# Sums of down weights made in the last phase, and another order of the closing products

## The reference, cut to what matters

```python
x = x + 0.5 * ffn(layernorm(x))          # x: 4 tiles of 512 tokens, D = 512
x = x + scan_block(layernorm(x))         # matmul, gated scan, layernorm
x = x + 0.5 * ffn(layernorm(x))

def ffn(x):                              # DIM_HIDDEN = 2048, the same weights both times
    gate, up = x @ w_gate.T, x @ w_up.T
    return (silu(gate) * up) @ w_down.T
```

## Time and profile before

| what | value |
|---|---|
| runs | 1024.21, 1025.92, 1026.52 us (median 1025.92) |
| profiled execution | 1023.93 us, span 1022.2 us |
| busy in the span | PE 1010.2, DVE 720.5, ACT 426.6, POOL 193.1 us |
| phases 0, 1, 2, 3 end at about | 260, 521, 783, 1019 us |
| granted clock | 1.000 |

### The profile page before, as it was taken

The page is one execution under the profiler, slowest core; times in us unless marked ns, Lnnn a source line. Parts: engine busy times, 40 slices in busy tenths (PEclk is TensorE's granted clock), DMA queues, the critical chain, the costliest instruction groups (busy, mean ns, idle before and its releaser), DMA issues.

```text
span 1022.2 us, 13275 instructions
## 1 busy us (share of the span) xinstructions
PE 1010.2 (99%) x4796; PEld 849.0 (83%) x4796; DVE 720.5 (70%) x1063; ACT 426.6 (42%) x681; POOL 193.1 (19%) x219
## 2 busy tenths in 40 slices
PE   8999999999999999999999999999999999999998
PEld 7778888877888888888888888888888888888998
DVE  7856685689888787866977887786586444454753
ACT  6645555547333632313824344232273332333530
POOL 4443365306300200210412020003040000000000
PEclk9999999999999999999999999999999999999999
DMA  6589998888666644646756764554577645554255
GB/s 206 205 320 348 358 343 299 311 273 258 231 234 231 221 145 165 208 150 226 250 181 221 234 223 161 180 168 145 182 267 242 216 166 200 209 178 165 94 182 179
DMA packets 73617, 224.21 MB, mean 219 GB/s; under 512 B 6481, under 2 KB 24913, under 8 KB 65873
## 3 DMA queue, kind: packets, MB, share of 16 engines
q1 hardware_dynamic: 72976, 222.33, 63.1%
q10 hardware_dynamic: 576, 1.05, 0.3%
HBM read 168.82 MB, written 54.53 MB: 219 GB/s over the span
## 4 chain that ended last, share of the span: by engine, by line
PE 92%; DVE 3%; DMA 2%; issue 1%; ACT 1%; SPq 1%; POOL 0%; DVEq 0%; ACTq 0%
PE ps_a L1779 8%; PE ps_a L1780 8%; PE ps_a L1781 8%; PE ps_b L1779 7%; PE ps_b L1780 7%; PE ps_b L1781 7%; PE ps_d L1779 7%; PE ps_d L1781 7%; PE ps_d L1780 7%; PE ps_c L1781 6%; PE ps_c L1780 6%; PE ps_c L1779 6%; PE aux L1779 3%; PE aux L1780 3%; PE aux L1781 3%; DMA t_kept<-zx 1%
## 5 line engine op out<-in xcount | busy, mean ns | idle before, releaser
L1203 DVE TENSOR_TENSOR tmp<-tmp,ps_c 128x512 f32<-128x512 f32 x59 | 40.4, 685 | 120.5 <-PE ps_c L1781 120.5
L1779 PE MATMUL ps_a<-xt,gu 128*128 128x512 f32 x304 | 118.4, 390 | 0.6 <-ACT tmp L707 0.6
L1780 PE MATMUL ps_a<-xt,gu 128*128 128x512 f32 x304 | 118.3, 389 | 0.0
L1781 PE MATMUL ps_a<-xt,gu 128*128 128x512 f32 x304 | 118.3, 389 | 0.0
L1779 PE MATMUL ps_b<-xt,gu 128*128 128x512 f32 x286 | 111.5, 390 | 1.3 <-ACT tmp L680 1.3
L1780 PE MATMUL ps_b<-xt,gu 128*128 128x512 f32 x286 | 111.3, 389 | 0.0
L1781 PE MATMUL ps_b<-xt,gu 128*128 128x512 f32 x286 | 111.3, 389 | 0.0
L1779 PE MATMUL ps_d<-dn,hid 128*128 128x512 f32 (+1 forms) x256 | 92.9, 363 | 0.5 <-DVE hid L1248 0.5
L1781 PE MATMUL ps_d<-dn,hid 128*128 128x512 f32 (+1 forms) x256 | 92.8, 363 | 0.0
L1780 PE MATMUL ps_d<-dn,hid 128*128 128x512 f32 (+1 forms) x256 | 92.8, 362 | 0.0
L1781 PE MATMUL ps_c<-xt,gu 128*128 128x512 f32 x236 | 91.8, 389 | 0.0
(11 more groups left out here) (272 smaller groups left out, 2321.2 us busy)
## 6 DMA issues: line engine op xcount, KB each, us to landing
dn<-dn_kept SPq DMA_DIRECT2D x92, 512.0 KB, 3.9
gu<-gu_kept SPq DMA_DIRECT2D x46, 1024.0 KB, 5.1
gu<-gu_kept SPq DMA_DIRECT2D x46, 768.0 KB, 5.1
gu_kept<-gu SPq DMA_DIRECT2D x14, 1024.0 KB, 5.7
gu_kept<-gu SPq DMA_DIRECT2D x14, 768.0 KB, 4.2
dn_kept<-dn SPq DMA_DIRECT2D x16, 512.0 KB, 5.2
t_kept<-zx SPq DMA_DIRECT2D x16, 512.0 KB, 5.8
dn<-t_kept SPq DMA_DIRECT2D x16, 512.0 KB, 3.6
```

The lines of the kernel that those rows point to most:

```text
L1203: dve.tensor_tensor(dst, u3s(si), p5_bank(si)[:, :], ALU.add).then_inc(c22_done, 1)
L1779: pe.matmul(dst, a_hi, b_hi, start=start, stop=False, skip_group_check=chained)
L1780: pe.matmul(dst, a_hi, b_lo, start=False, stop=False, skip_group_check=chained)
L1781: return pe.matmul(dst, a_lo, b_hi, start=False, stop=stop, skip_group_check=chained)
```

## The change

Four things change.

1. The T sums leave phase 0. They are made beside sets 2 to 9 of the last phase (one pair per set) from rows that are loaded again (`load_t_raw`, 512 KB a pair) into free rows of `zx`. POOL's, ACT's, DVE's and SP's parts all move; the store `keep_t` stands between `fetch_dn` and `fetch_b`. There is one buffer for raw rows and one for sums, so pair j waits for pair j-1.
2. `s_of` no longer makes s2; s4 is made in two steps from s3. DVE still has four instructions per pair. s2 is made by POOL, for two pairs at once, in four instructions of 128x1024 (`s2_of`), into `tmp`. `tmp` is in use until the last set's `gated12`, so `s2_of(0)` waits for that.
3. The batches stand in the order of `ENDING`: Q5 quarters 0 and 1, Q6 quarters 0 to 3, Q5 quarters 2 and 3, then Q7, Q3, Q4. The splits follow this order.
4. `d1_hi` no longer waits for the T sums in phase 0, and `load_dn_raw` no longer waits for them; the output stores of tiles 2 and 3 change places.

```diff
+    ENDING = ([(Q5, 0), (Q5, 1)] + [(Q6, i) for i in range(4)] + [(Q5, 2), (Q5, 3)]
+              + [(w, i) for w in (Q7, Q3, Q4) for i in range(4)])
...
+            def load_t_raw(j):
+                if j == 0:
+                    sp.wait_ge(d_done, SEG)
+                wait(sp, t_sums, 4 * j)
+                sp.dma_start(zx_rows[:, 0:2, :], w_ffn_in[2 * j:2 * j + 2, :, 2 * W:2 * W + D].rearrange(
+                    "h p n -> p h n")).then_inc(t_raw_arrived, 16)
...
+                    if p == LAST and 2 <= si < 1 + PAIRS:
+                        load_t_raw(si - 1)
                     if g + 2 < SETS * PH:
                         fetch_a(g + 2)
...
+                    if p == LAST and 2 <= si < 2 + PAIRS:
+                        keep_t(si - 2)
                     if g + 2 < SETS * PH:
                         fetch_b(g + 2)
...
             def d1_hi(p, m):
                 wait(act, d_done, 32 * p + 16 + m - 4 + 1 if m >= 4 else 32 * p)
-                if m < 2 and p == 0:
-                    act.wait_ge(t_lo, PAIRS)
-                if 2 <= m < 4 and p == 0:
-                    act.wait_ge(t_stored, 32 * PAIRS)
+                if m < 4 and p == 0:
+                    act.wait_ge(plain_done, 8)
...
                 act.wait_ge(s_step, 4 * (2 * i + 1) + (2 if w == Q5 else 4))
+                if w == Q6:
+                    act.wait_ge(s2_step, i + 1)
                 act.copy(xt[:, stage_op(n), 0, :, :], stage_rows(w, i)).then_inc(stage_hi, 1)
...
                     copy_u3(g)
+                    if p == LAST and si < 2 + PAIRS:
+                        t_hi_of(si - 2)
...
+            def s2_of(i):
+
+                pool.wait_ge(s_step, 4 * (2 * i + 2))
+                if i == 0:
+                    pool.wait_ge(hid1_done, 16 * PH)
+                    pool.wait_ge(hid21_done, 8 * PH)
+                pool.tensor_tensor(s2_rows(i), hid1[:, 4 * i + 1:4 * i + 4:2, :], first_rows(i, 0), ALU.subtract
+                                   ).then_inc(s2_step, 1)
...
+            for j in range(PAIRS):
+                t_sums_of(j)
+            for i in range(4):
+                s2_of(i)
...
-                dve.tensor_tensor(s2, tile1_odd, s3, ALU.subtract).then_inc(s_step, 1)
+                dve.tensor_tensor(s4, s4, s3, ALU.add).then_inc(s_step, 1)
                 dve.wait_ge(s_step, 4 * q + 3)
-                dve.tensor_tensor(s4, first_row(q, 1), s2, ALU.subtract).then_inc(s_step, 1)
+                dve.tensor_tensor(s4, s4, tile1_odd, ALU.subtract).then_inc(s_step, 1)
...
                 before_c12(p, si)
+                if p == LAST and si < 2 + PAIRS:
+                    t_lo_of(si - 2)
...
-                    pe.wait_ge(block_added, {Q6: 2, Q3: 6, Q7: 8, Q4: 12}[w])
+                    pe.wait_ge(block_added, {Q6: 2, Q3: 8, Q7: 6, Q4: 10}[w])
```

More of the change, by code:

```diff
@@ L255, in by_half, with s2_rows, t_raw @@
             return row.rearrange("p (a n) -> p a n", a=2)
-        def t_raw(j):
-            r = 4 * (j % 2)
-            return zx_rows[:, r:r + 2, :].rearrange("p r (a n) -> p (r a) n", a=2)
+        def s2_rows(i):
+            return tmp[:, 2 * i:2 * i + 2, :]
+        def t_raw():
+            return zx_rows[:, 4:6, :].rearrange("p r (a n) -> p (r a) n", a=2)
         def t_part(part):
@@ L498, in fetch_dn @@
                 else:
[L499 to L501 removed]
+                    w, i = ENDING[n - SEG - PAIRS]
+                    if n < SEG + PAIRS + 4:
+                        sp.wait_ge(t_stored, 32 * (2 * i + 2))
                     if w == Q3:
@@ L617, in _ @@
                     if si == 1:
+                        if p == LAST:
+                            load_t_raw(0)
                         for fetch in (fetch_a, fetch_b):
@@ L798, in t_hi_of @@
                 act.wait_ge(t_sums, 4 * j + 4)
-                if j == 0:
-                    act.wait_ge(plain_done, 8)
                 wait(act, t_stored, 32 * j)
-                act.copy(t_part(0), t_raw(j)).then_inc(t_hi, 1)
+                act.copy(t_part(0), t_raw()).then_inc(t_hi, 1)
             def zw_hi_of(j):
@@ L1006, in _ @@
                         dn_hi_of(si)
-                        if si % 2 == 0:
-                            t_hi_of(si // 2 - 1)
-                        if si == 15:
-                            t_hi_of(7)
                         if 5 <= si < 9:
@@ L1079, in t_sums_of @@
             def t_sums_of(j):
-                even, odd = dn_raw[:, 0, :], dn_raw[:, 1, :]
+                even, odd = zx_rows[:, 0, :], zx_rows[:, 1, :]
                 b11, b12, b21, b22 = even[:, 0:HALF], even[:, HALF:D], odd[:, 0:HALF], odd[:, HALF:D]
-                t = t_raw(j)
-                pool.wait_ge(dn_raw_arrived[0], 16 * (j + 1))
-                pool.wait_ge(dn_raw_arrived[1], 16 * (j + 1))
-                wait(pool, t_lo, j - 1)
+                t = t_raw()
+                pool.wait_ge(t_raw_arrived, 16 * (j + 1))
+                wait(pool, t_lo, j)
                 pool.tensor_tensor(t[:, 0, :], b12, b11, ALU.subtract).then_inc(t_sums, 1)
@@ L1156, in _ @@
                 sums(k)
-                if k % 2 == 0 and k <= SETS:
-                    t_sums_of(k // 2 - 1)
                 if k == 11:
@@ L1333, in add_product @@
             def add_product(w):
-                banks, tile, half, added = {Q5: (z_ps, 3, 1, 0), Q6: (x_ps, 2, 1, 0), Q3: (z_ps, 2, 1, 8),
-                                            Q7: (x_ps, 3, 1, 6), Q4: (x_ps, 3, 0, 0)}[w]
-                add_block(banks, 0, tile, half, bank_done, w + 1, added)
-                add_block(banks, 1, tile, half, batch_done, 4 * w + 4, added)
+                banks, tile, half, added = {Q5: (z_ps, 3, 1, 0), Q6: (x_ps, 2, 1, 0), Q3: (z_ps, 2, 1, 6),
+                                            Q7: (x_ps, 3, 1, 8), Q4: (x_ps, 3, 0, 0)}[w]
+                add_block(banks, 0, tile, half, bank_done, ENDED.index(w) + 1, added)
+                add_block(banks, 1, tile, half, batch_done, ENDING.index((w, 3)) + 1, added)
             def zw_lo_of(j):
@@ L1948, in first_block, with batch @@
                 last.then_inc(first_done, 1)
-            def batch(w, i):
-                m = 4 * w + i
+            def batch(m):
+                w, i = ENDING[m]
                 n = SEG + PAIRS + m
@@ L2139, in _ @@
                 first_block(PAIRS - 1, odd)
-            for w in (Q5, Q6, Q3, Q7, Q4):
-                for i in range(4):
-                    batch(w, i)
+            for m in range(len(ENDING)):
+                batch(m)
 def kernel(**inputs):
```

32 lines of the change are left out of this document (13 added, 19 removed).

## The result

| | before | after |
| --- | --- | --- |
| median of 20 runs each, us | 1023.80 (1022.34 to 1026.52) | 1026.01 (1025.37 to 1026.88) |
| the profiled execution's own time, us | 1023.93 | 1025.42 |
| its span, us | 1022.2 | 1023.6 |
| mean granted clock | 1.000 | 0.997 |
| PE, DVE, ACT, POOL busy, us | 1010.2, 720.5, 426.6, 193.1 | 1009.7, 726.9, 426.2, 201.1 |

The changed kernel takes 1.0021 of the time of the one before (95% interval 1.0015 to 1.0028), so it is 2.2 us slower. The forecast was 1029.5 us: 3.6 (0.35%) above the median of three runs that it started from, 5.7 above the kernel before as 20 runs have it. The direction was right, the size was not.

What follows compares the result with a forecast made beforehand. PE, busy 1010.2 of 1022.2 us, was taken as the bound. Terms -4.95 - 1.1 + 0 + 8.3 + 1.5 = +3.75 us gave 1029.5 us against the median 1025.92; range 1021.0 to 1033.0.

Steps and rivals of the forecast that it cites:

- Third set of phase 0: PE's wait there for ACT, itself held by the store of the pair before, goes: gain 1.5 us.
- last `lo0`: End of phase 0's sets: PE's 0.5 us wait, behind `t_lo` on DVE and `d1_hi` on ACT, goes: gain 0.75 us.
- `d1_lo`: End of phase 0: PE's two waits for its late fifth and sixth parts, 2.2 us, go: gain 2.7 us.
- Phase 0 together: Sum of the three gains in phase 0 from moving the T sums out: -4.95 us.
- Q7 and Q4: Last phase: they share banks and PE idles for the add; with Q3 between them, -1.1 us.
- Sets of the last phase: T sums beside these eight sets fall where DVE and ACT wait for PE: cost 0, bound 10 us.
- the store rival: Last phase: `t_hi_of(j)` waits for the store of j-1, 2 us in each of three sets: 1035.5 us; chance 0.1.
- The gap: Before the third batch, behind the last phase's sets: POOL's s2 instructions hold DVE in turns, PE waits: +8.3 us.
- rivals without the shutting-out: DVE and POOL don't block each other at 1024 elements, or POOL shares; split on time: 1021.1 us, faster; chance 0.12.
- with DVE first: DVE goes first at each hand-over to POOL; adds end +6.2 us, with the clock +7.7: 1027.5 us; chance 0.08.
- The clock: Behind the gap before the third batch PE returns at half clock: +1.5 us, bounds 0 and 1.7.
- The rival in which the clock stays up: DVE and POOL take turns as forecast, but PE's clock does not fall: sum +2.25, 1028.2 us; chance 0.2.

Runs made afterwards that it cites:

- s2 in pieces: Changed kernel with POOL's s2 in 16 instructions of 128x256 in place of four of 128x1024, at the same place: 1022.56 us, 0.9981 of the kernel before.
- the order by product: Changed kernel with each product's four batches in a row (Q5, Q6, Q3, Q7, Q4), so the third batch needs no s2: 1026.08 us, 1.0019 of the kernel before.

## Why the prediction was right or wrong

- **Third set of phase 0, 1.5; last `lo0`, 0.75; `d1_lo`, 2.7.** Each was right: from start to start the three places lost 1.5, 0.7 and 2.7 before, and nothing after. Nothing became late in their stead.
- **Phase 0 together, -4.95.** It was -6.2 by the books and -6.5 with the traces side by side. That is 1.3 to 1.6 too small, and the first failed step: "Behind the start, the waits that the change touches are few." I left out the wait of 0.57 us at 43 us (0.8 with the slow start behind it), because ACT's L707 has no T work near it; POOL's order had to be followed back 20 us to see it. The runs show that it is POOL's eight instructions in a row: with four of them left out it goes, with their order changed it stays. Gaps of 0.1 us in the second half of phase 0, 0.4 together, went too.
- **Q7 and Q4, -1.1.** Right: 1.1 in the trace; 0.9 to 1.3 for the order alone.
- **Sets of the last phase, 0.** Right, and the store rival is refuted: the store of `t_kept` lands in 6.2 us at most, ACT waited for it once, for 0.3 us. (The median of 4.5 us in the earlier trace rows was misread: that answer has the loads from `t_kept` among the stores. The 16 stores of before alone have a median of 5.8, those of after 4.8.)
- **The gap, +8.3.** Right in mechanism, with 7.8 lost. Of its marks one was badly put: POOL's L1110 reads 2.8 to 3.3 us and not 2.4, since its own wait for the turn is in it. 2.4 us a turn were 2.2, since only 0.54 and not 0.60 of a 256-element instruction holds DVE. Three turns of 0.2 make the difference of 0.5. The rivals without the shutting-out (L1333 would be 0.7) and with DVE first (6.2) are refuted.
- **The clock, +1.5.** Right in kind, but 1.8 in the trace is above the bound of 1.7, and 2.7 in another profile far above it: PE does not always come back as it came from the start. The rival in which the clock stays up is refuted by 0.50 in the row above.
- **The sum, +3.75.** By the books it should have been +2.3: 1.3 too little gained in phase 0, 0.5 too much in the gap, 0.3 too little for the clock.
- **From the sum to the time.** The second failed step: "That execution lies 2.0 below the median of the runs shown, so against the median 1025.92 I say 1029.5 us". The median of three runs was 2.1 above that of twenty (1023.80), while the profiled execution (1023.93) was at it. With its own base the sum gives 1027.7, and the right sum 1026.2. Why the three runs lay so high isn't shown, as their clocks aren't on record; in 69 later executions of this kernel the mean granted clock was 0.998 in five, the two slowest (1026.32 and 1026.24 us) among them.

The direction came out right, but not quite for the reason given. I had the gap alone, 8.3 us, outweigh a gain of 6.05. The gap was 7.8 and the gain 7.3 by the books (7.6 side by side), which is nearly even; it is the slow clock behind the gap that made the kernel slower, and with PE kept at work through the gap the difference to the kernel before was gone (0.9996, 0.9987 to 1.0005). So the clock's term decided the sign; in my sum the gap did so by itself. The number itself can't tell the forecast from its rivals: with the right base the rival whose clock stays up would stand at 1026.2, next to the 1026.01 measured, and only the rows refute it.

## What to carry to other kernels

When work is moved to an idle POOL, price it by what DVE does beside it: here each DVE instruction with two SBUF inputs waited for a whole one of POOL, 2.2 us at 1024 elements and 0.54 at 256. So give POOL small instructions, and let it start behind the DVE work that PE waits for. A stall that ends with a transfer's landing can swallow what is gained ahead of it, as the 0.86 us here, so mend that one first. When gain and loss are nearly even, the small terms set the sign. And take the base of a forecast from as many executions as there are; three can be off by as much as the effect.

## What the runs showed of the hardware

- **DVE and POOL take strict turns.** With both at work without a break, DVE's 128x512 subtraction takes 0.69 us alone, 1.23 beside POOL's 128x256 and 2.86 beside its 128x1024. A DVE instruction of 1024 elements (1.22 alone) takes 2.19 with one such POOL instruction and 3.42 with another, as it happens to meet one.

  The Trainium skill (SBUF — State Buffer, "Who interferes with whom") has it that the two shut each other out for the whole instruction. The trace agrees at 1024 elements too, where no row of before had shown it, and adds the amounts: 0.54 and 2.2 us a turn.
- **DVE's adds of banks stay out of it.** Two `SCALAR_TENSOR_TENSOR` from `ps_d` take 1.28 beside POOL's 1024 elements, as without POOL.
- **The clock also fell behind shorter waits of PE.** With s2 in pieces it read 0.50 from 964.0 to 966.5 us behind a wait of 4.35 (the matmuls 0.21 apart, 1.5 us lost). Without the first pair's T sums it read 0.50 from 78.25 to 81.25 us behind one of 2.43, where PE had been back for over 1 us. In the profile of the kernel before it read 1.00 behind 1.26 at the same place. The runs don't tell what decides between these.
- **The slow stretch has no fixed length.** From PE's return to the clock's rise it was 3.8 us in the changed kernel (1.8 lost) and 5.9 in the order by product (2.7 lost), behind gaps of 7.9 and 6.7 us from start to start.
